# Layer 2 of a two-layer recurrent model: scaling of the gelu rows and their negative mean from VectorE to ScalarE, clipping later in VectorE's order

## The chip, the cores and the metric

The kernel runs on one core of a Trainium2 chip. The metric is the device time of one execution in microseconds, the median of several runs. TensorE multiplies matrices and transposes, VectorE, ScalarE and GpSimd work on rows, and SyncE's queue starts most transfers.

## What is computed

Two layers over 2048 tokens (2 x 1024) of width 256. Layer 1 is an attention with a mixture of 64 experts beside it. Layer 2 is a small attention whose output is gated by a feed-forward net with quantised activations. The part that matters here is that net:

```python
def absmax_quant(x):
    gamma = jnp.max(jnp.abs(x), axis=-1, keepdims=True)
    x_hat = jnp.clip(x * Q_B / gamma, -Q_B + EPS, Q_B - EPS)
    return x_hat * gamma / Q_B

def bitlinear(x, w):
    xn = layer_norm(x)
    x_hat = absmax_quant(xn)          # straight-through form left out
    w_hat = ternarize_weights(w)
    return jnp.einsum('bsd,od->bso', x_hat, w_hat)

h = bitlinear(x, w_fc)                # 256 -> 1024
h = jax.nn.gelu(h, approximate=False)
return bitlinear(h, w_proj)           # 1024 -> 256
```

Then `x = x + s * silu(ffn)`. The 1024-wide rows after gelu are normalised, scaled by 128 over their largest magnitude, clipped at 128 and multiplied with ternary weights.

## The kernel before

The program has one hand-written instruction list for each engine, and semaphores between them. There is no scheduler: the order is that of the code. Up to some 303 us of the profiled execution it works on layer 1; what follows is layer 2.

Layer 2 takes the 16 tiles of 128 tokens in pairs, p = 0 to 7 (`NP` = 8, `GT` = 2 tiles each). Every engine runs the loop `for p in range(NP + 2)` with several stages in flight. For one pair the stages are these, with the lines of the profile:

- GpSimd adds up the layer-1 result: `total` (line 467), `add_gated` (473, 474), signal `x1_ready`.
- VectorE normalises and quantises the 256-wide rows: `moments` (1115 to 1123), and `scales_and_rows`, which mixes Newton steps for reciprocal square roots (1094 to 1102) with the row steps `quantise` (1136 to 1147). Line 1147 is the last, with the signal `xq_ready`. It works two pairs ahead.
- TensorE transposes (`turn_q`, 1524), ScalarE copies the upper half to 16 bits (`high_q`, 713), VectorE takes the rest (`low_q`, 1174), and TensorE multiplies (`qkv`, 1538, `fc`, 1547).
- ScalarE computes gelu with a row sum (732) into `hid`. VectorE makes the negative mean (`means`, 1184), ScalarE squares the centred rows with a row sum (`square`, 738), VectorE takes their maximum (`spreads`, 1190, 1191) and, after the Newton steps, the scale and the bias (`hidden_scales`, 1194 to 1203).
- VectorE scales and shifts `hid` in place (`quantise_hidden`, 1211, two tiles) and clips it (1214, two tiles, signal `clip_ready`).
- ScalarE rounds to 16 bits (`high_hidden`, 753), GpSimd subtracts to get the rest (`low`, 502), TensorE transposes both (`turn_hidden`, 1576), ScalarE copies them out (`take_hT`, 745, 746), and TensorE multiplies (`down1`, 1587).
- ScalarE takes a tanh (`gate2`, 783), VectorE the product (`silu2`, 1221), GpSimd the last product and sum (`finish`, 510, 511), and SyncE stores.
- The small attention lies beside it: GpSimd `score_products` (483 to 489) and `attend` (496, 498), VectorE 1179, ScalarE 759, 763, 776, and TensorE `turn_att` (1558) and `project` (1566).

GpSimd's order in a round is: `total`, `attend`, `finish` twice, `add_gated`, `score_products`, `low` twice. ScalarE's ends with `take_hT`, two squares and two `high_hidden`. VectorE's is: line 1179, `spreads`, `moments`, `scales_and_rows`, `hidden_scales`, `silu` (1108), `means`, `quantise_hidden`, `product_scales`, `low_q`.

Of the kernel before, what the change touches and what calls it, by code (L numbers as in the profile page):

```python
# [54 lines left out]
GT = 2  # L55
# [18 lines left out]
def build(nc, q, Wk, bk, Wv, bv, Wo, bo, rw, eb, wg, wu, wd, sg, su, sd, wqkv, wpo, wfc, wpj, out):  # L74
# [9 lines left out]
    with ExitStack() as ctx:  # L84
# [107 lines left out]
        def l1(n):  # L192
# [88 lines left out]
                             "hi_ready", "lo_ready", "hT1_ps", "hT1_ready")]  # L281
        clip_ready = sem("clip_ready")
        z_ps, ztanh_ready, zu_ready, out_ready, out_stored = [sem(n) for n in (
# [254 lines left out]
        def _(sc):  # L538
# [187 lines left out]
            def gelu(n):  # L726
# [3 lines left out]
                if n >= 2 * GT:  # L730
                    sc.wait_ge(lo_ready, n - 2 * GT + 1)
                sc.activation(hid[n // GT % 2][:, q_, :], two[1][:, :], ACT.Gelu, scale=fcscale[n // GT % 2][:, q_:q_ + 1],  # L732
                              accum_out=hsum[:, q_:q_ + 1]).then_inc(gelu_ready, 1)

            def square(n):
                q_ = n % GT
                sc.wait_ge(nmean_ready, n // GT + 1)
                sc.activation(sq[q_], hid[n // GT % 2][:, q_, :], ACT.Square, bias=nmean[:, q_:q_ + 1], scale=1.0,
                              accum_out=ssq[:, q_:q_ + 1]).then_inc(sq_ready, 1)
# [57 lines left out]
            high_q(1)  # L797
            gelu(1)
            for q_ in range(GT):
                square(q_)  # L800
            for p in range(NP + 2):
# [23 lines left out]
                if p < NP:  # L825
                    for q_ in range(GT):
                        if p + 1 < NP:
                            square(GT * (p + 1) + q_)
                    for q_ in range(GT):
                        high_hidden(GT * p + q_)  # L830

        @block.vector
        def _(ve):
# [346 lines left out]

            def means(p):
                ve.wait_ge(gelu_ready, GT * p + GT)
                ve.wait_ge(dve, step[0])
                ve.tensor_scalar(nmean[:, :], hsum[:, :], -1.0 / FF1, None, ALU.mult).then_inc(nmean_ready, 1)

            def spreads(p):
# [6 lines left out]
            def hidden_scales(p):  # L1193
                mark(ve.tensor_scalar(hscale[:, :], ny[:, 3 * GT:], QB, None, ALU.mult))
                got = mark(ve.tensor_tensor(tmpc[:, :], nv[:, 3 * GT:], ny[:, 3 * GT:], ALU.mult))
                ve.wait_ge(dve, got - 1)
                mark(ve.tensor_tensor(hbias[:, :], hscale[:, :], nmean[:, :], ALU.mult))
                ve.wait_ge(dve, got)

                if p >= 2:  # L1200
                    ve.wait_ge(ztanh_ready, GT * (p - 1))
                    ve.wait_ge(s1_ready, p - 1)
                ve.scalar_tensor_tensor(out=zhalf[p % 2][:, :], in0=tmpc[:, :], scalar=gwc[:, 1:2], in1=ny[:, 2 * GT:3 * GT],
                                        op0=ALU.mult, op1=ALU.mult).then_inc(zhalf_ready, 1)

            def quantise_hidden(p):

                rows = [hid[p % 2][:, q_, :] for q_ in range(GT)]
                ve.wait_ge(dve, step[0])
                for q_, h in enumerate(rows):  # L1210
                    last = mark(ve.tensor_scalar(h, h, hscale[:, q_:q_ + 1], hbias[:, q_:q_ + 1], ALU.mult, ALU.add))  # L1211
                ve.wait_ge(dve, last)
                for h in rows:
                    ve.tensor_scalar(h, h, QB, -QB, ALU.min, ALU.max).then_inc(clip_ready, 1)
# [22 lines left out]
            low_q(1)  # L1237
            means(0)
            for p in range(NP + 2):
# [8 lines left out]
                if p + 3 < NP:  # L1248
                    silu(p + 3)
                if p + 1 < NP:  # L1250
                    means(p + 1)
                if p < NP:
                    quantise_hidden(p)
                if p + 2 < NP:
                    product_scales(p + 2)
                    low_q(p + 2)
                if p >= NP:
                    for q_ in range(GT):
# [382 lines left out]
```

## Time and profile before

| what | us |
|---|---|
| median of three runs | 491.08 |
| the three runs | 488.03, 491.08, 493.98 |
| span of the profiled execution, first to last instruction | 487.5 |
| VectorE busy in the span | 323.2 (66%) |
| GpSimd busy | 311.5 (64%) |
| ScalarE busy | 242.7 (50%) |
| TensorE busy | 374.0 (77%) |

The profiled execution's own device time is not given beside its span. The span is of one execution, the median of three others or the same. Busy time counts an instruction from its start to its end, whatever it does in between. A timeline row gives the start, the time taken, the engine, the line and what is written from what; an idle time and what ended it stand in brackets.

### The profile page before, as it was taken

Reading aid. Unit: us, or ns where it says so; the run is one execution under the profiler, and the core shown is the slowest. Engines: PE = TensorE matmul, PEld = TensorE weight load, DVE = VectorE, ACT = ScalarE, POOL = GpSimd, SP = SyncE. Lnnn points to the kernel's source line nnn. Section 1 sums busy time; section 2 is a strip of 40 time slices with the busy share of each in tenths; the row PEclk is TensorE's granted clock in tenths of the full one; section 3 lists DMA queues with packets and bytes.
Section 4 is the critical chain, followed back from the end, with each engine's and each line's share of the span. In section 5 each row is a group of like instructions: output and inputs, shape, how many; then the busy total and the mean of one; then the engine's idle time right before and its main releaser. Section 6 shows DMA issues by size and latency. Waiting matters only on the chain.

```text
span 487.5 us, 7393 instructions
## 1 busy us (share of the span) xinstructions
PE 374.0 (77%) x2246; PEld 282.0 (58%) x2246; DVE 323.2 (66%) x924; ACT 242.7 (50%) x542; POOL 311.5 (64%) x306
## 2 busy tenths in 40 slices
PE   0999969779998978978998973266676876779673
PEld 0974435566786756867786852133464663556562
DVE  6629892656555443556475631578999999999930
ACT  1344332624343436433344432327686967879661
POOL 6440005277877776788888874733957966968872
PEclk9999986899999999999899999678898989999797
DMA  7940055978889999778788556800000000000000
GB/s 250 339 136 0 1 150 185 274 178 182 211 178 209 244 226 217 144 167 181 159 202 179 94 68 109 281 0 0 2 0 11 13 24 1 23 22 12 13 32 32
DMA packets 58873, 57.90 MB, mean 119 GB/s; under 512 B 7099, under 2 KB 56531, under 8 KB 58835
## 3 DMA queue, kind: packets, MB, share of 16 engines
q1 hardware_dynamic: 46547, 38.55, 26.5%
q0 software_dynamic: 12288, 18.88, 21.1%
q8 instruction: 18, 0.29, 0.3%
q14 instruction: 20, 0.16, 0.1%
HBM read 39.69 MB, written 17.73 MB: 118 GB/s over the span
## 4 chain that ended last, share of the span: by engine, by line
DVE 33%; PE 30%; issue 12%; DMA 11%; POOL 8%; ACT 3%; SPq 1%; POOLq 0%; ACTq 0%; DVEq 0%
DMA acc_d<-W,idxE 7%; DVE W L1211 4%; DVE nv L1190 3%; PE two L1447 3%; POOL acc_d L459 3%; PE two L1307 3%; PE two L1363 3%; PE two L1273 3%; PE two L1459 2%; DMA W<-tok_d,idxE 2%; DVE nv L1191 2%; PE two L1399 2%; POOL W L439 2%; PE two L1321 2%; PE two L1436 2%
## 5 line engine op out<-in xcount | busy, mean ns | idle before, releaser
L459 POOL DMA_INDIRECT acc_d<-W,idxE x64 | 102.3, 1599 | 28.5 <-issue 14.8
L439 POOL DMA_INDIRECT W<-tok_d,idxE x56 | 56.6, 1010 | 61.4 <-DMA tok_d<-F 44.6
L1056 DVE SCALAR_TENSOR_TENSOR W<-W,two 128x88 f32<-128x88 f32 x64 | 15.6, 244 | 58.7 <-ACT W L679 35.4
L663 ACT ACTIVATE W<-two 128x256 f32<-128x256 f32 x64 | 24.4, 382 | 52.9 <-PE two L1436 50.8
L1547 PE MATMUL two<-wfcT,F 128*128 128x512 f16 x128 | 31.8, 393 | 6.3 <-ACT W L732 6.3
L502 POOL TENSOR_TENSOR F<-W,F 128x1024 f16<-128x1024 f32 x16 | 33.8, 2131 | 3.0 <-ACT F L753 2.4
L1033 DVE TENSOR_SCALAR W<-two,W 128x256 f32<-128x256 f32 x56 | 26.8, 479 | 12.6 <-DMA acc_d<-W,idxE 4.7
L1399 PE MATMUL two<-A,v 128*128 128x128 f32 x256 | 31.5, 276 | 4.4 <-issue 4.1
L1436 PE MATMUL two<-ident,W 128*128 128x128 f32 x112 | 24.0, 297 | 13.8 <-DMA W<-tok_d,idxE 11.1
L1399 PEld LDWEIGHTS two<-A,v 128*128 128x128 f32 x256 | 30.7, 192 | 6.3 <-issue 5.7
L1436 PEld LDWEIGHTS two<-ident,W 128*128 128x128 f32 x112 | 19.2, 201 | 25.7 <-DMA W<-tok_d,idxE 16.5
L1447 PE MATMUL two<-W 128*128 128x176 f32 x160 | 31.9, 324 | 0.2 <-ACT W L670 0.2
L1363 PE MATMUL two<-kT,vT 128*128 128x512 f32 x64 | 30.8, 604 | 0.0
L1587 PE MATMUL two<-wpjT,F 128*128 128x256 f16 x256 | 30.5, 280 | 0.0
L930 DVE TENSOR_REDUCE nmax<-two 128x1 f32<-128x1024 f32 x16 | 19.6, 1224 | 15.8 <-PE two L1363 13.8
L1587 PEld LDWEIGHTS two<-wpjT,F 128*128 128x128 f16 x256 | 25.7, 101 | 4.3
L510 POOL TENSOR_TENSOR F<-F 128x256 f32<-128x256 f32 x16 | 11.6, 727 | 22.8 <-DVE F L1221 22.8
L1459 PE MATMUL two<-W 88*128 88x256 f32 x80 | 25.1, 396 | 1.3 <-DVE W L1033 0.9
L1447 PEld LDWEIGHTS two<-W 128*128 128x128 f32 x160 | 25.4, 200 | 0.7 <-issue 0.7
L1576 PE MATMUL two<-ident,F 128*128 128x128 f16 x256 | 20.5, 244 | 5.8 <-POOL F L502 3.7
L1547 PEld LDWEIGHTS two<-wfcT,F 128*128 128x128 f16 x128 | 12.0, 101 | 20.1 <-ACT W L732 8.1
L1576 PEld LDWEIGHTS two<-ident,F 128*128 128x128 f16 x256 | 18.8, 111 | 8.2 <-POOL F L502 4.2
(230 smaller groups left out, 1035.3 us busy)
## 6 DMA issues: line engine op xcount, KB each, us to landing
acc_d<-xn SPq DMA_DIRECT2D x8, 512.0 KB
W<-in_L_ffn_w_gate SPq DMA_DIRECT2D x20, 176.0 KB
W<-in_L_ffn_w_up SPq DMA_DIRECT2D x20, 176.0 KB
W<-in_L_ffn_w_down SPq DMA_DIRECT2D x20, 176.0 KB
F<-in_L_ffn_w_gate SPq DMA_DIRECT2D x12, 176.0 KB
F<-in_L_ffn_w_up SPq DMA_DIRECT2D x12, 176.0 KB
F<-in_L_ffn_w_down SPq DMA_DIRECT2D x12, 176.0 KB
x<-in_L_attn_q SPq DMA_DIRECT2D x4, 512.0 KB, 5.6
```

The costliest lines, as they stand in the source:

```text
L439: pool.indirect_dma_start(out=xg[n % XR], out_offset=None, in_=tok_d[:, :], in_offset=bass.IndirectOffsetOnAxis(ap=idxE[:, n:n + 1], axis=0))\
L459: pool.indirect_dma_start(out=acc_d[n % 2][:, :], out_offset=bass.IndirectOffsetOnAxis(ap=idxE[:, n:n + 1], axis=0), in_=ysb[n % YS], in_o ...
L502: pool.tensor_tensor(lo16[n % GT], hid[n // GT % 2][:, n % GT, :], hi16[n % GT], ALU.subtract)\
L1033: ve.tensor_scalar(ysb[n % YS], bk_(3)[:, 0:D], xg[n % XR][:, D + n:D + n + 1], 0.5, ALU.mult, ALU.mult)\
L1363: ins = pe.matmul(two[2][:, 512 * h:512 * h + 512], vT[:, rows], kT[:, at:at + 512], start=True, stop=True)
L1399: ins = pe.matmul(bk_(1)[:, 0:P], v[:, (ORDER[t] // NP) * NP + i, :], probT[t % 2][:, i, :], start=(i == 0), stop=(i == 7))
L1436: ins = pe.transpose(bk_(2)[:, P * k:P * k + P], xg[n % XR][:, 0:D].rearrange("p (n k) -> p k n", k=KH)[:, k, :], ident[:, :])
L1447: ins = pe.matmul(gu[n % 2].rearrange("p (m f) -> p m f", m=2), xgT[n % 2][:, k, :], wgu[r][:, n % WG, :, k, :], start=(k == 0), stop=(k = ...
L1459: pe.matmul(bk_(3)[:, 0:D], hT[n % 2], wdn[(n // WG) % WR][:, n % WG, :], start=True, stop=True)\
L1547: ins = pe.matmul(bk_(2 + h), part[:, n % GT, k, :], wfcT[:, k, 512 * h:512 * h + 512], start=(i == 0), stop=(i == 3))
L1576: ins = pe.transpose(bk_(b).bitcast(F16)[:, P * k:P * k + P], part[n % GT][:, P * k:P * k + P], ident16[:, :])
L1587: ins = pe.matmul(bk_(7)[:, D * (n % GT):D * (n % GT) + D], part[n % 2][:, P * k:P * k + P], wpjT[:, k, :], start=(i == 0), stop=(i == 2 * ...
```

## The change

In layer 2, ScalarE gets two new steps. `scale_hidden` scales and shifts a tile of `hid` in place with one activation, once VectorE signals `hbias_ready`. `means` forms the negative mean there. VectorE's `quantise_hidden` only clips, each tile once `u_ready` says that it is scaled, and it stands after `product_scales` and `low_q` instead of before. The squares of the next pair follow ScalarE's new steps.

```diff
--- before.py
+++ after.py
@@ -279,7 +279,7 @@
         fc_ps, gelu_ready, nmean_ready, sq_ready, zhalf_ready, hi_ready, lo_ready, hT1_ps, hT1_ready = [
             sem(n) for n in ("fc_ps", "gelu_ready", "nmean_ready", "sq_ready", "zhalf_ready",
                              "hi_ready", "lo_ready", "hT1_ps", "hT1_ready")]
-        clip_ready = sem("clip_ready")
+        clip_ready, hbias_ready, u_ready = [sem(n) for n in ("clip_ready", "hbias_ready", "u_ready")]
         z_ps, ztanh_ready, zu_ready, out_ready, out_stored = [sem(n) for n in (
             "z_ps", "ztanh_ready", "zu_ready", "out_ready", "out_stored")]
 
@@ -732,9 +732,21 @@
                 sc.activation(hid[n // GT % 2][:, q_, :], two[1][:, :], ACT.Gelu, scale=fcscale[n // GT % 2][:, q_:q_ + 1],
                               accum_out=hsum[:, q_:q_ + 1]).then_inc(gelu_ready, 1)
 
+            def means(p):
+
+                sc.wait_ge(gelu_ready, GT * p + GT)
+                sc.activation(nmean[:, :], hsum[:, :], ACT.Copy, scale=-1.0 / FF1).then_inc(nmean_ready, 1)
+                sc.wait_ge(nmean_ready, p + 1)
+
+            def scale_hidden(n):
+
+                q_ = n % GT
+                sc.wait_ge(hbias_ready, n // GT + 1)
+                h = hid[n // GT % 2][:, q_, :]
+                sc.activation(h, h, ACT.Identity, bias=hbias[:, q_:q_ + 1], scale=hscale[:, q_:q_ + 1]).then_inc(u_ready, 1)
+
             def square(n):
                 q_ = n % GT
-                sc.wait_ge(nmean_ready, n // GT + 1)
                 sc.activation(sq[q_], hid[n // GT % 2][:, q_, :], ACT.Square, bias=nmean[:, q_:q_ + 1], scale=1.0,
                               accum_out=ssq[:, q_:q_ + 1]).then_inc(sq_ready, 1)
 
@@ -796,6 +808,7 @@
             gelu(0)
             high_q(1)
             gelu(1)
+            means(0)
             for q_ in range(GT):
                 square(q_)
             for p in range(NP + 2):
@@ -824,7 +837,10 @@
                     take_hT(GT * (p - 1) + 1)
                 if p < NP:
                     for q_ in range(GT):
-                        if p + 1 < NP:
+                        scale_hidden(GT * p + q_)
+                    if p + 1 < NP:
+                        means(p + 1)
+                        for q_ in range(GT):
                             square(GT * (p + 1) + q_)
                     for q_ in range(GT):
                         high_hidden(GT * p + q_)
@@ -1178,11 +1194,6 @@
                 ve.wait_ge(prod_ready, p + 1)
                 ve.tensor_reduce(dif[:, :].rearrange("p (g r) -> p g r", r=REP1), pr, AX.X, ALU.add).then_inc(dif_ready, 1)
 
-            def means(p):
-                ve.wait_ge(gelu_ready, GT * p + GT)
-                ve.wait_ge(dve, step[0])
-                ve.tensor_scalar(nmean[:, :], hsum[:, :], -1.0 / FF1, None, ALU.mult).then_inc(nmean_ready, 1)
-
             def spreads(p):
 
                 for q_ in range(GT):
@@ -1194,7 +1205,8 @@
                 mark(ve.tensor_scalar(hscale[:, :], ny[:, 3 * GT:], QB, None, ALU.mult))
                 got = mark(ve.tensor_tensor(tmpc[:, :], nv[:, 3 * GT:], ny[:, 3 * GT:], ALU.mult))
                 ve.wait_ge(dve, got - 1)
-                mark(ve.tensor_tensor(hbias[:, :], hscale[:, :], nmean[:, :], ALU.mult))
+                ve.wait_ge(nmean_ready, p + 1)
+                ve.tensor_tensor(hbias[:, :], hscale[:, :], nmean[:, :], ALU.mult).then_inc(hbias_ready, 1)
                 ve.wait_ge(dve, got)
 
                 if p >= 2:
@@ -1205,12 +1217,9 @@
 
             def quantise_hidden(p):
 
-                rows = [hid[p % 2][:, q_, :] for q_ in range(GT)]
-                ve.wait_ge(dve, step[0])
-                for q_, h in enumerate(rows):
-                    last = mark(ve.tensor_scalar(h, h, hscale[:, q_:q_ + 1], hbias[:, q_:q_ + 1], ALU.mult, ALU.add))
-                ve.wait_ge(dve, last)
-                for h in rows:
+                for q_ in range(GT):
+                    h = hid[p % 2][:, q_, :]
+                    ve.wait_ge(u_ready, GT * p + q_ + 1)
                     ve.tensor_scalar(h, h, QB, -QB, ALU.min, ALU.max).then_inc(clip_ready, 1)
 
             def silu2(n):
@@ -1235,7 +1244,6 @@
                     silu(2)
                     low_q(0)
             low_q(1)
-            means(0)
             for p in range(NP + 2):
                 if p < NP:
                     score_difference(p)
@@ -1247,13 +1255,11 @@
                     hidden_scales(p)
                 if p + 3 < NP:
                     silu(p + 3)
-                if p + 1 < NP:
-                    means(p + 1)
-                if p < NP:
-                    quantise_hidden(p)
                 if p + 2 < NP:
                     product_scales(p + 2)
                     low_q(p + 2)
+                if p < NP:
+                    quantise_hidden(p)
                 if p >= NP:
                     for q_ in range(GT):
                         silu2(GT * (p - 2) + q_)
```

VectorE's order around the clip, in one of the middle rounds, before. `W` holds the gelu rows, `F` the smaller tiles, `two` is PSUM:

```order
L1197 TENSOR_TENSOR hbias<-hscale,nmean 128x2 [waits dve_seq]
L1203 SCALAR_TENSOR_TENSOR zhalf<-tmpc,gwc,ny 128x2 [waits s1_ready,ztanh_ready,dve_seq]
L1108 SCALAR_TENSOR_TENSOR F<-F,xn 128x512 [waits gate_ready]
L1184 TENSOR_SCALAR nmean<-hsum 128x2 [waits dve_seq,gelu_ready]
L1211 TENSOR_SCALAR W<-W,hscale,hbias 128x1024 [waits dve_seq]
L1211 TENSOR_SCALAR W<-W,hscale,hbias 128x1024
L1214 TENSOR_SCALAR W<-W 128x1024 [waits dve_seq]
L1214 TENSOR_SCALAR W<-W 128x1024
L1167 SCALAR_TENSOR_TENSOR kvscale<-amax,ny 128x2 [waits gelu_ready,qkv_ready]
L1169 SCALAR_TENSOR_TENSOR fcscale<-amax,gwc,ny 128x2
L1174 TENSOR_TENSOR F<-two,F 128x512 [waits qT_hi_ready]
```

and after the change, at the same place (lines below 735 move down by 10 to 16, so 1124 is the old 1108 and 1223 the old 1214):

```order
L1209 TENSOR_TENSOR hbias<-hscale,nmean 128x2 [waits nmean_ready,dve_seq]
L1215 SCALAR_TENSOR_TENSOR zhalf<-tmpc,gwc,ny 128x2 [waits s1_ready,ztanh_ready,dve_seq]
L1124 SCALAR_TENSOR_TENSOR F<-F,xn 128x512 [waits gate_ready]
L1183 SCALAR_TENSOR_TENSOR kvscale<-amax,ny 128x2 [waits gelu_ready,qkv_ready]
L1185 SCALAR_TENSOR_TENSOR fcscale<-amax,gwc,ny 128x2
L1190 TENSOR_TENSOR F<-two,F 128x512 [waits qT_hi_ready]
L1223 TENSOR_SCALAR W<-W 128x1024 [waits u_ready] x2
L1195 TENSOR_REDUCE dif<-F 128x16 [waits prod_ready]
L1201 TENSOR_REDUCE nv<-W 128x1 [waits sq_ready] x2
```

The two scalings and the mean are gone; the product scales and low_q come first, and the clips wait for `u_ready` right ahead of the next round's first instruction.

ScalarE's order at the end of a round, before:

```order
L745 ACTIVATE F<-two 128x1024 [waits z_ps,hT1_ps]
L746 ACTIVATE F<-two 128x1024
L738 ACTIVATE W,ssq<-W,nmean 128x1024 [waits nmean_ready] x2
L753 ACTIVATE F<-W 128x1024 [waits hT1_ps,clip_ready] x2
L759 ACTIVATE F<-F 128x256 [waits attT_ps]
```

and after (738 and 746 are the new mean and scaling; 750, 757, 758 and 765 the old 738, 745, 746 and 753):

```order
L757 ACTIVATE F<-two 128x1024 [waits z_ps,hT1_ps]
L758 ACTIVATE F<-two 128x1024
L746 ACTIVATE W<-W,hbias,hscale 128x1024 [waits hbias_ready] x2
L738 ACTIVATE nmean<-hsum 128x2 [waits gelu_ready]
L750 ACTIVATE W,ssq<-W,nmean 128x1024 [waits nmean_ready]
L750 ACTIVATE W,ssq<-W,nmean 128x1024
L765 ACTIVATE F<-W 128x1024 [waits hT1_ps,clip_ready] x2
```

Two scalings and a mean stand between the copies of the transposed rows and the squares; the squares and the roundings to 16 bits come after them.

## Rows read from the trace of the kernel before

**Rows 1.** The page's slices: VectorE's busy tenths in 40 equal parts of the span.

```profile
DVE  6629892656555443556475631578999999999930
```

**Rows 2.** Busy time in one full round of the second layer.

```profile
core 0: us, PE busy (x) PEld busy (x) DVE busy (x) ACT busy (x) POOL busy (x), PEclk, DMA share, GB/s
384.70:404.70 20.00, 14.91 (x108) 11.22 (x108) 19.79 (x45) 14.85 (x26) 16.07 (x17) 0.91 0.05 15
```

**Rows 3.** VectorE in that round, in order of time: start us, us taken, then what.

```profile
387.17 1.94 DVE L1191 TENSOR_SCALAR nv<-ssq 128x2 f32<-128x2 f32 x1
...
391.03 0.82 DVE L1136 TENSOR_SCALAR F<-x,mv 128x256 f32<-128x256 f32 x1
...
394.08 0.43 DVE L1147 TENSOR_SCALAR F<-F 128x512 f32<-128x512 f32 x1
...
398.36 1.84 DVE L1211 TENSOR_SCALAR W<-W,hscale,hbias 128x1024 f32<-128x1024 f32 x1
```

**Rows 4.** Line 1191 in the round from 330 us.

```profile
L1191 DVE TENSOR_SCALAR nv<-ssq x1: 159/159/159, 334.0 to 334.0; 128x2 f32<-128x2 f32 x1
```

**Rows 5.** GpSimd from 384 us on, in order of time.

```profile
384.86 4.23 POOL L502 TENSOR_TENSOR F<-W,F 128x1024 f16<-128x1024 f32 x2
...
390.97 0.73 POOL L498 TENSOR_TENSOR F<-F 128x256 f32<-128x256 f32 x1
...
404.86 4.22 POOL L502 TENSOR_TENSOR F<-W,F 128x1024 f16<-128x1024 f32 x2
```

**Rows 6.** Line 1147 in three other rounds.

```profile
338.22 0.43 DVE L1147 TENSOR_SCALAR F<-F 128x512 f32<-128x512 f32 x1
...
356.15 0.43 DVE L1147 TENSOR_SCALAR F<-F 128x512 f32<-128x512 f32 x1
...
432.42 0.43 DVE L1147 TENSOR_SCALAR F<-F 128x512 f32<-128x512 f32 x1
```

**Rows 7.** Line 502 in four other rounds.

```profile
346.93 4.21 POOL L502 TENSOR_TENSOR F<-W,F 128x1024 f16<-128x1024 f32 x2
...
440.21 4.23 POOL L502 TENSOR_TENSOR F<-W,F 128x1024 f16<-128x1024 f32 x2
...
454.36 4.21 POOL L502 TENSOR_TENSOR F<-W,F 128x1024 f16<-128x1024 f32 x2
...
467.40 4.21 POOL L502 TENSOR_TENSOR F<-W,F 128x1024 f16<-128x1024 f32 x2 [2.45 <-ACT F L753]
```

**Rows 8.** ScalarE in order of time; in brackets its idle time before.

```profile
341.00 1.14 ACT L738 ACTIVATE W<-W,nmean 128x1024 f32<-128x1024 f32 x1
...
360.48 1.15 ACT L738 ACTIVATE W<-W,nmean 128x1024 f32<-128x1024 f32 x1
...
385.05 0.20 ACT L763 ACTIVATE td<-dif 128x16 f32<-128x16 f32 x1
...
399.97 1.15 ACT L738 ACTIVATE W<-W,nmean 128x1024 f32<-128x1024 f32 x1
...
436.75 1.15 ACT L738 ACTIVATE W<-W,nmean 128x1024 f32<-128x1024 f32 x1
...
439.01 2.00 ACT L753 ACTIVATE F<-W 128x1024 f16<-128x1024 f32 x2
...
452.96 2.00 ACT L753 ACTIVATE F<-W 128x1024 f16<-128x1024 f32 x2 [0.23 <-DVE W L1214]
...
463.81 1.02 ACT L746 ACTIVATE F<-two 128x1024 f16<-128x1024 f16 x1
466.26 2.00 ACT L753 ACTIVATE F<-W 128x1024 f16<-128x1024 f32 x2 [1.44 <-DVE W L1214]
```

**Rows 9.** TensorE's lines 1524 and 1576 after idle time, in order of time.

```profile
394.56 0.99 PE L1524 MATMUL two<-ident,F 128*128 128x128 f32 x4 [3.38 <-DVE F L1147]
...
432.90 0.65 PE L1524 MATMUL two<-ident,F 128*128 128x128 f32 x4 [2.54 <-DVE F L1147]
...
456.54 1.89 PE L1576 MATMUL two<-ident,F 128*128 128x128 f16 x16 [2.37 <-POOL F L502]
```

## The prediction

> **What bounds the kernel now.** I read the page's slices first: VectorE reads 9 in almost every slice from 330 to 466 us [rows 1]. That is the second layer, so an edit that takes work off VectorE looks right. The busy times of one round say more: in 20.00 us VectorE is busy 19.79, GpSimd 16.07, ScalarE 14.85 [rows 2]. Then I read VectorE in order of time, and its busy time turns out to hold waits. Line 1191 works on two numbers per partition; it takes 0.159 us in the first round [rows 4] and 1.94 us here [rows 3]. Here it ends at 389.11, and GpSimd's pair of line 502 ends at 389.09 [rows 5]. Line 1136, 0.82 us, ends at 391.85, GpSimd's line 498 at 391.70. So a VectorE instruction of this sort stands still until GpSimd's current instruction is over.
>
> The Trainium skill, SBUF — State Buffer, "Who interferes with whom", says that the two engines share a pair of ports as an exclusive lock, whoever starts first holding it for its whole instruction; the trace agrees (1.94 against 0.159 us). It names tensor_scalar and operations with two SBUF inputs as the VectorE side.
>
> This splits a round into two legs. Leg one runs from the first line 502 (the "low" subtraction, 384.86) to the end of line 1147 (394.51), which gives TensorE the next rows: 9.65 us, of the same length one round earlier (346.93 [rows 7] to 356.58 [rows 6]). It goes by GpSimd's string: two line 502, line 467, 496, 498; VectorE can do little until they are through. Taking work off VectorE leaves this leg as it is. Leg two runs from the end of line 1147 to the next line 502: 394.51 to 404.86 is 10.35 us. Line 502 needs ScalarE's line 753, and GpSimd must be through its own list.
>
> **The change, leg two by leg two.** S is the time from the end of line 1147 to ScalarE's first square (line 738); the two scalings go in there. Removed from VectorE per round: two line 1211 at 1.84 us or less (part of it waiting) and line 1184. Added to ScalarE ahead of the squares: two 1024-wide scalings and a two-element mean that the engine waits for itself. No row has a scaling with both scale and bias from memory. From below it is the plain line 753, two in 2.00 us, so 1.0 each. From above, and nearest in form, the squares: 436.75 to 439.01 is 2.26 for two [rows 8], 1.13 each. I take 1.13. The mean is like line 763, 0.20 us, plus about 0.1 (my estimate, half of that row) for the engine's wait on its own result: 0.3. Sum 2.56, lower end 2.2, upper end 2.9 (a tenth more for each scaling, twice the wait).
>
> The Trainium skill, ScalarE: Activation LUTs, "What ACT_TABLE_LOAD costs", gives 186 + 0.833 N ns, 93 more per pointer operand, 93 less back to back. With N = 1024 and two pointers that is an estimate of 1.13 us; with the plain copy's price the sum below would be some 2.5 us smaller.
>
> After S come 2.56 (new), 2.26 (squares) and then line 753 to line 502, which took 466.26 to 467.40 = 1.14. Line 502 is due at S + 5.96, by rows 8 and 7. The clip of line 1214, now after each scaling, waits beside the squares and hides there. The early product scales and low_q let TensorE start qkv and fc sooner; it waits for other things, so they cost nothing and bring ScalarE about 0.2 us once where its list is full. GpSimd's own list filled leg two to 10.35 us while it stood behind line 1211 and others. With one such wait (1.84 [rows 3]) gone it ends at 8.5, with none at 10.35. I take it to be under ScalarE's 9.9, since line 1211 came twice a round; at the upper end the three gains of 0.45 below are lost and the sum is 1.35 larger.
>
> - First leg two: S = 341.00 - 338.65 = 2.35 [rows 6, 8]; due at 8.31, was 8.28. Nothing.
> - Second: S = 360.48 - 356.58 = 3.90; due at 9.86, was 8.29: +1.6.
> - Third and fourth: was 10.35 each (the rows of the fourth stand for both). S was 399.97 - 394.51 = 5.46 with TensorE's line 1524 at 0.99 us after 3.38 idle, that is at 1.2 GHz; in the round of 432.90 it took 0.65 after 2.54 idle, at 2.4 GHz [rows 9], and S was 3.90. After the change I count some 2.6 us of idle ahead of it (fc now starts when gelu allows, and gelu moves with the squares). At 2.4 GHz: due at 9.9, -0.45 each. At 1.2 GHz: 11.4, +1.05 each.
> - Fifth: S as at 2.4 GHz: -0.45.
> - Sixth: end of line 1147 at 432.85; S = 436.75 - 432.85 = 3.90; due at 9.86. It was 440.21 - 432.85 = 7.36, because GpSimd has a short list: +2.5.
> - Seventh round (440.21 to 454.36): ScalarE had been busy from the line 753 at 439.01 to that at 452.96 but for little (0.23 before the latter). It gets 2.56 more, less that 0.23 and the 0.2 from above; line 502 then follows at once rather than behind GpSimd's list: +1.9 to 2.1.
> - Last round: line 746 ends at 464.83, line 753 started 466.26, 1.4 to 1.5 behind; now two scalings, 2.26: +0.7. Scaling and clipping overlap, but the first line 753 stands behind both scalings in ScalarE's order.
> - Before the first round, the first mean no longer crosses to VectorE and back: -0.2, an estimate from line 763's 0.20 us in rows 8.
>
> Sum at 2.4 GHz: 0 + 1.6 - 0.9 - 0.45 + 2.5 + 2.0 + 0.7 - 0.2 = +5.2. At 1.2 GHz in the third and fourth: +8.2. 2.6 us of idle lies close to the 2.54 that kept the clock, but line 1576 after 2.37 of idle ran its sixteen in 1.89 us, where the clock was low; I go a quarter of the way, +5.9. The span was 487.5 us; the profiled execution's own time isn't given apart, the lowest of the three runs is 488.03, the median 491.08. The addition lies wholly in the second layer, so I put it on the median: 497.0.
>
> **Rivals.** (a) Cheap scalings: 2.2 instead of 2.56, 0.36 less in the six leg twos that ScalarE ends and 0.26 in the last: +5.2 - 2.4 = +2.8, 493.9. For it: line 753. Against it: the squares have one operand from memory and take 0.13 more each.
> (b) Low clock in the third and fourth round: +8.2, 499.3. For it: 3.38 idle did it before, 2.37 may. Against it: gaps get shorter there.
> (c) VectorE sets the pace, and leg one shrinks. If its small instructions get through between GpSimd's, what leaves it is gained up to ScalarE's own pace: 14.85 + 2.56 = 17.4 a round. The five rounds from 346.93 to 440.21 took 93.3; five of 17.4 are 87.1: -6.2. The last two still give +2.0 + 0.7, the first -0.2: -3.7, 487.4, not slower and up to 1% faster. It decides from the point where VectorE reaches line 1136 before GpSimd's string starts. For it: 19.79 busy of 20.00. Against it: the pairs of equal ends in rows 3 and 5. The Trainium skill, Perfetto Trace Analysis, "Optimizing Scalar/DVE Operations", holds that moving work to ScalarE may pay if VectorE is saturated; that is this case, and whether VectorE is saturated or standing is what decides. Its ScalarE page, "Rules for kernel authors", says against the change that multiplies and adds belong on VectorE.
>
> **How the numbers follow.** The main case 0.42, own range 494.5 to 499; (a) 0.24; (b) 0.16; (c) 0.16; 0.02 for what I don't see. A measurement here tells about 1% from no change, 4.9 us. Slower by more: (b) and four fifths of the main case, 0.50. Faster by more: half of (c) and the rest, 0.10. The remainder 0.40 is within 1%. The range runs from (c) to just past (b): 488.5 to 500.
>
> **What would show it.** Right: line 1191 still ends with a line 502; leg one stays 9.65 us; the first line 502 starts about 9.9 us after line 1147 in every leg two from the second to the sixth; ScalarE's idle time after 440 us is gone; the scaling takes about 1.2 us from start to end. Wrong: leg one falls to 8 us or less (then (c)), or scalings near 1.05 us (then (a)), or line 1524 at 0.99 us (then (b)). The forecast fails as a whole if GpSimd's line 502 starts earlier in leg two than it did before in the sixth round.

## The result and the profile after

The changed kernel takes 496.24 us (median of four runs, 495.09 to 497.99) against 490.16 us for the kernel before, a ratio of 1.0113 with a 95% interval of 1.0079 to 1.0146. The forecast was 497.0, 5.9 us above the 491.08 known then. The change costs 5.5 us by the ratio and 6.1 by the two medians, just over 1%. The profiled execution took 495.68 us, its span 493.9. Ratios leave out single executions far slower than the others: among the twelve of the second measurement in experiment 1 one took 2008.79 us, which its median of 488.96 still counts (488.57 without it).

The page of the changed kernel, with the busy times and VectorE's slices:

```profile
PE 379.4 (77%) x2246; PEld 286.6 (58%) x2246; DVE 311.3 (63%) x900; ACT 260.2 (53%) x566; POOL 303.0 (61%) x306
...
DVE  6629991745554354656676540858969999986920
```

VectorE's busy time went from 323.2 to 311.3 us, ScalarE's rose from 242.7 to 260.2, and in VectorE's slices the unbroken row of nines [rows 1] now has eights and a six in it. VectorE got its relief and the kernel got slower.

The rounds, from GpSimd's first line 502 (the lower halves of the scaled rows) to the next. The timeline's columns are start, time taken, engine, line, output and input, and in brackets the idle time before and what ended it:

```profile
347.21 4.21 POOL L502 TENSOR_TENSOR F<-W,F 128x1024 f16<-128x1024 f32 x2 [0.18 <-ACT F L765]
...
367.72 4.21 POOL L502 TENSOR_TENSOR F<-W,F 128x1024 f16<-128x1024 f32 x2 [4.71 <-ACT F L765]
...
386.87 4.21 POOL L502 TENSOR_TENSOR F<-W,F 128x1024 f16<-128x1024 f32 x2 [0.37 <-ACT F L765]
...
407.01 4.21 POOL L502 TENSOR_TENSOR F<-W,F 128x1024 f16<-128x1024 f32 x2 [1.26 <-ACT F L765]
...
425.12 4.21 POOL L502 TENSOR_TENSOR F<-W,F 128x1024 f16<-128x1024 f32 x2 [0.37 <-ACT F L765]
...
443.23 4.21 POOL L502 TENSOR_TENSOR F<-W,F 128x1024 f16<-128x1024 f32 x2 [3.80 <-ACT F L765]
...
460.49 4.20 POOL L502 TENSOR_TENSOR F<-W,F 128x1024 f16<-128x1024 f32 x2 [4.97 <-ACT F L765]
...
474.23 4.21 POOL L502 TENSOR_TENSOR F<-W,F 128x1024 f16<-128x1024 f32 x2 [3.68 <-ACT F L765]
```

Where [rows 5] and [rows 7] had no wait ahead of line 502 but in the last round, now there is one in every round, and it is for ScalarE's line 765, the old 753. The other end of a leg is VectorE's line 1163, the old 1147, here in the timeline of the changed kernel, to be held against [rows 6] (those of 395.72 and 414.83 look the same):

```profile
339.11 0.43 DVE L1163 TENSOR_SCALAR F<-F 128x512 f32<-128x512 f32 x1
...
356.07 0.43 DVE L1163 TENSOR_SCALAR F<-F 128x512 f32<-128x512 f32 x1
...
376.58 0.43 DVE L1163 TENSOR_SCALAR F<-F 128x512 f32<-128x512 f32 x1
...
432.94 0.43 DVE L1163 TENSOR_SCALAR F<-F 128x512 f32<-128x512 f32 x1
```

Leg two runs from the end of such a row to the next line 502, leg one from there to the end of the next such row. With both sets of rows:

| | leg two before | after | my due time | leg one after it, before | after |
|---|---|---|---|---|---|
| first | 8.28 | 7.67 | 8.3 | 9.65 | 9.29 |
| second | 8.29 | 11.22 | 9.9 | 9.65 | 9.29 |
| third | 10.35 | 9.86 | 9.9 | 9.65 | 9.28 |
| fourth | 10.35 | 10.86 | 9.9 | 8.82 | 8.25 |
| fifth | 10.35 | 9.86 | 9.9 | 8.82 | 8.25 |
| sixth | 7.36 | 9.86 | 9.9 | | |

Round seven (443.23 to 460.49) takes 17.26 us, it was 14.15; the last (to 474.23) 13.74, it was 13.04. The legs two add 4.35 us, the legs one take away 2.23, the last two rounds add 3.81; the first line 1163 here ends 0.89 us later than the first line 1147 there, and what follows the last line 502 is 0.4 shorter. That makes the 6.4 us between the two spans. The 0.89 us lie ahead of the first added scaling (341.25), and such differences come without a cause in the code: in two profiles of one kernel (experiment 1) the first leg two starts at 338.75 and at 339.42, and its second and third line 1147 lie 15.09 and 13.90 us apart.

ScalarE's list in the sixth leg two of the changed kernel, and its wait in round seven:

```profile
437.27 2.37 ACT L746 ACTIVATE W<-W,hbias,hscale 128x1024 f32<-128x1024 f32 x2
439.54 0.20 ACT L738 ACTIVATE nmean<-hsum 128x2 f32<-128x2 f32 x1
439.76 1.15 ACT L750 ACTIVATE W<-W,nmean 128x1024 f32<-128x1024 f32 x1
...
442.05 1.99 ACT L765 ACTIVATE F<-W 128x1024 f16<-128x1024 f32 x2
...
451.08 1.11 ACT L732 ACTIVATE W<-two,fcscale 128x1024 f32<-128x1024 f32 x1 [1.54 <-issue]
```

The scalings start at 437.27, 3.90 us after line 1163 ended; that is S. Two scalings and the mean reach to the squares at 439.76, 2.49 (I had 2.56), the squares to 442.05, 2.29 (2.26), and line 502 follows at 443.23, 1.18 (1.14). Together 5.96, the number of the forecast. The rows of [rows 8] stood in the same order without the first two. The Trainium skill (ScalarE: Activation LUTs, "What ACT_TABLE_LOAD costs") has 186 + 0.833 N ns, 93 more for each pointer operand and 93 less back to back, from which 1.13 us for each scaling is an estimate. The trace agrees: from the first scaling to the mean's start it is 2.27 us for the two.

### The profile page after: what moved, and what is told of

Its sections match the earlier page's. It is cut to its first block and busy times, and to the rows that moved or that the text cites. A ratio compares the mean times of both kernels' runs of the same rounds, so it can differ in the third digit from the quotient of the medians.

```text
span 493.9 us, 7393 instructions
## 1 busy us (share of the span) xinstructions
PE 379.4 (77%) x2246; PEld 286.6 (58%) x2246; DVE 311.3 (63%) x900; ACT 260.2 (53%) x566; POOL 303.0 (61%) x306
## 5 line engine op out<-in xcount | busy, mean ns | idle before, releaser
L1553 PE MATMUL two<-wfcT,F 128*128 128x512 f16 x128 | 34.7, 420 | 11.7 <-ACT W L732 11.7
L1405 PE MATMUL two<-A,v 128*128 128x128 f32 x256 | 33.0, 284 | 6.4 <-issue 6.3
L1405 PEld LDWEIGHTS two<-A,v 128*128 128x128 f32 x256 | 32.0, 199 | 8.4 <-issue 7.8
L1582 PE MATMUL two<-ident,F 128*128 128x128 f16 x256 | 21.7, 252 | 17.6 <-POOL F L502 15.5
L1442 PEld LDWEIGHTS two<-ident,W 128*128 128x128 f32 x112 | 19.7, 201 | 21.7 <-DMA W<-tok_d,idxE 10.5
L946 DVE TENSOR_REDUCE nmax<-two 128x1 f32<-128x1024 f32 x16 | 19.6, 1223 | 16.3 <-PE two L1369 16.3
L510 POOL TENSOR_TENSOR F<-F 128x256 f32<-128x256 f32 x16 | 11.6, 724 | 20.4 <-DVE F L1230 20.4
```

Source lines behind the costliest of these rows:

```text
L1405: ins = pe.matmul(bk_(1)[:, 0:P], v[:, (ORDER[t] // NP) * NP + i, :], probT[t % 2][:, i, :], start=(i == 0), stop=(i == 7))
L1442: ins = pe.transpose(bk_(2)[:, P * k:P * k + P], xg[n % XR][:, 0:D].rearrange("p (n k) -> p k n", k=KH)[:, k, :], ident[:, :])
L1553: ins = pe.matmul(bk_(2 + h), part[:, n % GT, k, :], wfcT[:, k, 512 * h:512 * h + 512], start=(i == 0), stop=(i == 3))
L1582: ins = pe.transpose(bk_(b).bitcast(F16)[:, P * k:P * k + P], part[n % GT][:, P * k:P * k + P], ident16[:, :])
```

## The experiments

All ratios are to the kernel before, with runs of both on the same chip. The diffs are the parts that matter; new spare tiles and definitions are left out. A kernel goes by the number of its experiment. In the texts on record a kernel goes by its label, which stands in the heading of its experiment.

**1. The order alone (e1_order_only, and again e10_order_again).** This is the kernel before with another order. The scaling stays on VectorE; only the clip and the scaling move behind the product scales and low_q.

```diff
-                if p < NP:
-                    quantise_hidden(p)
                 if p + 2 < NP:
                     product_scales(p + 2)
                     low_q(p + 2)
+                if p < NP:
+                    quantise_hidden(p)
```

> The kernel before, with only VectorE's order changed: the scaling and the clip stay on VectorE but stand behind product_scales and low_q. Theory (ScalarE's list and TensorE's clock set the time from line 1147 to line 502): VectorE's clip ends about 1.3 us later, GpSimd's own list still fills 10.35 us in the third to fifth leg two, so those stay; the sixth goes from 7.4 to about 8.2 us. Total 0 to +2 us, ratio 1.000 to 1.004. Rival (VectorE's place in the chain is what counts, and the new order is what costs): most of the change's +6 us, ratio 1.008 or more.

Measured: 487.70 us, ratio 0.9947 (0.9897 to 0.9998). A second measurement beside another kernel:

> The kernel of e1_order_only once more, beside e9_hybrid_fill on the same chip, for the size of the order's gain. Theory: leg one 9.3 and 8.26 us, ratio to before 0.992 to 0.998. Rival: no gain, ratio 0.999 to 1.002, and the first measurement was chance.

Measured: 488.96 us, ratio 0.9943 (0.9906 to 0.998). So half of the change is a gain of half a per cent, which neither theory had. The legs two are nearly those of the kernel before (8.15, 8.16, three of 10.34, 7.88): the middle ones stay, as expected, and the sixth is 0.52 longer, where 0.8 was expected. The gain is in leg one: 9.30 and 8.26 instead of 9.65 and 8.82, as in the changed kernel. VectorE's timeline of this kernel in leg one:

```profile
385.81 0.36 DVE L1191 TENSOR_SCALAR nv<-ssq 128x2 f32<-128x2 f32 x1
...
390.18 0.82 DVE L1136 TENSOR_SCALAR F<-x,mv 128x256 f32<-128x256 f32 x1
...
392.88 0.43 DVE L1147 TENSOR_SCALAR F<-F 128x512 f32<-128x512 f32 x1
```

and GpSimd's:

```profile
384.01 4.22 POOL L502 TENSOR_TENSOR F<-W,F 128x1024 f16<-128x1024 f32 x2
...
390.11 0.73 POOL L498 TENSOR_TENSOR F<-F 128x256 f32<-128x256 f32 x1
```

Line 1191 takes 0.36 us here and ends as the first of the two line 502 is over (384.01 and 2.13 us later is 386.14, row end 386.17). Before, it started 2.31 us into the pair and stood until the second was over, 1.94 us [rows 3, 5]. The statistics of the next rows now lie beside the second line 502, and everything behind them comes earlier in VectorE's list. At the end of GpSimd's line 498 (390.84) it is the second of the two lines 1136 that comes free (ends 391.00), where before it was the first. The short one, 0.34 us, is done by then.

The changed kernel shows the same, VectorE first:

```profile
387.99 1.03 DVE L1202 TENSOR_SCALAR nv<-ssq 128x2 f32<-128x2 f32 x1
...
392.25 0.78 DVE L1152 TENSOR_SCALAR F<-x,mv 128x256 f32<-128x256 f32 x1
...
393.02 0.82 DVE L1152 TENSOR_SCALAR F<-x,mv 128x256 f32<-128x256 f32 x1
```

and the GpSimd row at which the last of them ends:

```profile
392.96 0.74 POOL L498 TENSOR_TENSOR F<-F 128x256 f32<-128x256 f32 x1
```

**2. Is it the lead that matters? (e8_late_reduce)** Kernel 1 with a maximum over 512 elements on VectorE ahead of line 1179, so that VectorE comes 0.6 us later.

```diff
                 if p < NP:
+                    ve.tensor_reduce(spare[:, p:p + 1], wpoT[:, :, :].rearrange("p k d -> p (k d)"), AX.X, ALU.max)
                     score_difference(p)
```

> The kernel of e1_order_only, with one more maximum over 512 elements (0.69 us) on VectorE ahead of line 1179 in each round. Theory (leg one is shorter in e1_order_only because VectorE reaches line 1191 before the first line 502 is over): that lead is lost, line 1191 stands until the second line 502 is over and leg one goes back to 9.65 and 8.82 us: +0.35 in the first four, +0.57 in the next, about 2 us over e1_order_only, ratio to before 0.997 to 1.001. Rival (leg one is VectorE's own work): +0.6 in every leg one, 3.5 us or more. Second rival (the lead doesn't matter): no change.

Measured: 491.78 us, ratio 1.0046 (1.0013 to 1.0078). Legs one are 9.63, 9.64, 9.64, 8.81 and 8.80. VectorE's timeline (its lines are one further down):

```profile
386.12 0.67 DVE L1242 TENSOR_REDUCE spare<-wpoT 128x1 f32<-128x512 f32 x1
...
389.30 1.86 DVE L1192 TENSOR_SCALAR nv<-ssq 128x2 f32<-128x2 f32 x1
...
393.07 0.82 DVE L1137 TENSOR_SCALAR F<-x,mv 128x256 f32<-128x256 f32 x1
...
396.12 0.43 DVE L1148 TENSOR_SCALAR F<-F 128x512 f32<-128x512 f32 x1
```

GpSimd's pair of line 502 in the same round:

```profile
386.91 4.22 POOL L503 TENSOR_TENSOR F<-W,F 128x1024 f16<-128x1024 f32 x2
```

The added instruction comes at 386.12, line 1191 (here 1192) starts 2.39 us into the pair and takes 1.86 again. 0.6 us of delay gave back 0.34 in the three longer legs and 0.55 in the two shorter ones. The rival had 0.6 in every leg; the shorter legs hardly tell the two apart, the longer ones do: there it is the place in GpSimd's string that counts. The total alone would have spoken for the rival: it is 4.1 us above the order alone by the medians and 4.9 by the ratios, where I expected 2. In the profiles the legs one add 2.1 us, and the sixth leg two another 0.97 (8.85 us, S at 5.40, TensorE at 1.2 GHz). Whether the delay had to do with that clock, and where the rest lies, stays open.

**3. The scalings left out (e2_no_scaling).** The changed kernel with one-element copies in place of ScalarE's two scalings, so the gelu rows aren't scaled.

```diff
-                sc.activation(h, h, ACT.Identity, bias=hbias[:, q_:q_ + 1], scale=hscale[:, q_:q_ + 1]).then_inc(u_ready, 1)
+                sc.activation(zlast[:, n:n + 1], hbias[:, q_:q_ + 1], ACT.Copy).then_inc(u_ready, 1)
```

> The kernel after, with ScalarE's two 1024-wide scalings replaced by one-element copies; the scaling of the gelu rows is left out. VectorE's and GpSimd's lists are those of the kernel after. Theory: 2.1 us less ahead of the squares in each round, so the sixth leg two falls from 9.9 to 7.8 us and round seven and the last fall by 2 each; the middle ones stop at GpSimd's list (8.5 to 9.5 us). Total 8 to 12 us below the kernel after, ratio to before 0.986 to 0.995. Rival (a) that the extra time of the change comes from VectorE's new waits and order: within 2 us of the kernel after, ratio 1.008 to 1.014.

Measured: 485.43 us, ratio 0.9876 (0.9828 to 0.9924), 10.8 us below the changed kernel by the medians and 11.6 by the ratios. ScalarE's list of the sixth leg two (its line 766 is the rounding):

```profile
433.50 0.30 ACT L747 ACTIVATE zlast<-hbias 128x1 f32<-128x1 f32 x2
...
433.92 1.15 ACT L751 ACTIVATE W<-W,nmean 128x1024 f32<-128x1024 f32 x1
...
436.20 1.99 ACT L766 ACTIVATE F<-W 128x1024 f16<-128x1024 f32 x2
```

GpSimd's line 502 after it:

```profile
437.39 4.22 POOL L503 TENSOR_TENSOR F<-W,F 128x1024 f16<-128x1024 f32 x2 [1.27 <-ACT F L766]
```

Line 1163 had ended at 429.60, so this leg two is 7.79 us, the expected 7.8. The third to fifth are 9.56 or 9.57 and no less, though ScalarE was ready: that is GpSimd's own list without the scalings on VectorE. The second is 9.15 with S at 5.26. Round seven falls by 3.4 us and the last by 1.3, where I expected 2 for each. VectorE's and GpSimd's lists are those of the changed kernel, so what the change costs is ScalarE's work.

**4. One scaling more (e3_third_scaling).** The changed kernel with a third scaling into a spare tile.

```diff
                         scale_hidden(GT * p + q_)
+                    sc.activation(spare[:, :], sq[1], ACT.Identity, bias=hbias[:, 1:2], scale=hscale[:, 1:2])
```

> The kernel after, with a third 1024-wide scaling into a spare tile on ScalarE in each round. Theory: +1.13 us in each leg two from the second to the sixth, in round seven and in the last, 0 to 1.1 in the first: +7 to +9 us over the kernel after, ratio to before 1.026 to 1.032. Rival (VectorE sets the pace, ScalarE has idle time in every round that takes it): 0 to +2 over the kernel after, ratio 1.011 to 1.016.

Measured: 507.27 us, ratio 1.0321 (1.0275 to 1.0367), 11.0 us above the changed kernel by the medians and 10.2 by the ratios. ScalarE's sixth leg two:

```profile
444.53 2.37 ACT L747 ACTIVATE W<-W,hbias,hscale 128x1024 f32<-128x1024 f32 x2
...
447.92 0.20 ACT L739 ACTIVATE nmean<-hsum 128x2 f32<-128x2 f32 x1
...
450.43 1.99 ACT L766 ACTIVATE F<-W 128x1024 f16<-128x1024 f32 x2
```

and GpSimd's line 502:

```profile
451.61 4.21 POOL L503 TENSOR_TENSOR F<-W,F 128x1024 f16<-128x1024 f32 x2 [5.72 <-ACT F L766]
```

From the first scaling to the mean is 3.39 us instead of 2.27, and from there to line 502 nothing changes (7.08 in all, 5.96 and 1.12). The first and the third leg two, with TensorE's clock as in the changed kernel, are 1.14 and 1.13 longer. The fifth and sixth are 1.6 longer: S is 4.35 and 4.40 there, behind a slow second fc (3.17 us for seven of its matmuls, 3.59 for eight). Round seven is 19.43 us, 2.2 longer. The total is 1 to 2 us over my 7 to 9. In the profiles the stretch from the first line 1163 to the last line 502 is 8.7 us longer, inside the forecast, and 3.0 us more lie ahead of it (342.51 against 339.54), before the first of the added scalings (346.49); what made those stays open. So ScalarE's time, which seemed free with 14.85 busy of 20 us [rows 2], is paid for at its full price.

**5. TensorE kept busy (e4_fill).** In the changed kernel, three places where TensorE stood idle read:

```profile
356.55 1.12 PE L1530 MATMUL two<-ident,F 128*128 128x128 f32 x4 [2.61 <-DVE F L1163]
...
396.21 0.66 PE L1530 MATMUL two<-ident,F 128*128 128x128 f32 x4 [2.39 <-DVE F L1163]
...
397.28 1.91 PE L1582 MATMUL two<-ident,F 128*128 128x128 f16 x16
...
447.76 3.23 PE L1553 MATMUL two<-wfcT,F 128*128 128x512 f16 x8 [1.29 <-ACT W L732]
```

Line 1530 (the old 1524) took 1.12 us in the second round. In the fourth it took 0.66, but the clock fell right behind it: it is 0.91 of the full one from 396.00 to 397.20 and 0.50 from 397.30 to 399.00, and line 1582 took 1.91 us for its sixteen, where the sixth leg two has 1.06. Line 1553 took 3.23 us for eight in round seven, where 1.89 is usual. The granted clock by round:

```profile
core 0: us, PE busy (x) PEld busy (x) DVE busy (x) ACT busy (x) POOL busy (x), PEclk, DMA share, GB/s
347.20:367.70 20.50, 15.45 (x107) 11.78 (x108) 15.44 (x41) 16.23 (x27) 11.25 (x12) 0.83 0.00 1
407.00:425.10 18.10, 13.91 (x113) 9.90 (x112) 17.31 (x41) 16.85 (x29) 14.10 (x15) 1.00 0.05 16
443.20:460.50 17.30, 12.05 (x87) 8.42 (x85) 12.88 (x24) 15.72 (x27) 10.38 (x14) 0.90 0.05 16
```

It is 0.83 of the full clock in the second round and 0.90 in round seven. The third and fourth rounds have 0.91 and 0.92, the fifth (shown) and the sixth 1.00. The experiment adds eight transposes of the identity at each of three places.

```diff
                 if 1 <= p <= NP:
+                    fill(8)
                     turn_hidden(GT * (p - 1))
                 if p + 1 < NP:
+                    fill(8)
                     fc(GT * (p + 1) + 1)
+                if p < NP:
+                    fill(8)
```

> The kernel after, with 8 transposes of the identity matrix on TensorE at each of three places where it stood idle (before turn_hidden, before the second fc, before turn_q). Theory: TensorE stays at 2.4 GHz, S in the second leg two falls from 5.3 to about 3.9 us, in the fourth from 4.9 to 3.9, and the second fc of round seven from 3.2 to 1.9 us: 3 to 4 us below the kernel after, less up to 1 us where a filler stands in the way, ratio to before 1.003 to 1.008. Rival (the lower clock is met by other slack): 0 to +2 us over the kernel after, ratio 1.011 to 1.016.

Measured: 493.58 us, ratio 1.0042 (1.001 to 1.0074), 3.5 us less than the changed kernel by the ratios. Two of its stretches, with the same columns:

```profile
349.10:368.30 19.20, 14.67 (x125) 11.38 (x124) 15.49 (x41) 16.17 (x27) 12.27 (x13) 1.00 0.01 1
443.10:459.50 16.40, 13.61 (x119) 11.16 (x117) 12.82 (x24) 15.80 (x27) 10.70 (x13) 1.00 0.05 17
```

The clock is full in the second to the seventh round, the second to sixth legs two are 9.85 or 9.86 all five, and round seven is 16.46. My main case had 16.1 for it and nothing but 9.9 for the legs: this is the kernel that I had computed. The two profiled executions alone don't show the gain: the spans are 494.1 and 493.9. From the first line 1163 to the last line 502 it is 3.25 us less, but the first line 1163 ends 1.9 us later and what follows the last line 502 is 1.6 us longer (21.2 against 19.7). That the fillers cost that 1.6 isn't shown; kernel 6, with the same fillers, has 20.1.

**6. Roundings first (e5_round_first_fill).** Kernel 5, with ScalarE's roundings ahead of the mean and the squares.

```diff
+                    for q_ in range(GT):
+                        high_hidden(GT * p + q_)
                     if p + 1 < NP:
                         means(p + 1)
                         for q_ in range(GT):
                             square(GT * (p + 1) + q_)
-                    for q_ in range(GT):
-                        high_hidden(GT * p + q_)
```

> The kernel of e4_fill (the change plus fillers on TensorE), with ScalarE's roundings (line 753 of before) ahead of the mean and the squares instead of behind them. Theory (line 502 starts a fixed stretch of ScalarE's list after S): the roundings start at S + 2.3, line 502 at S + 3.5 or at the end of GpSimd's own list: second leg two 9.9 to about 8, third to fifth 9.9 to 9.5, sixth 9.9 to 7.5 or 8; leg one back to 9.6 and 8.8, since the maxima come later. Together 3 to 4 us below e4_fill, ratio to before 0.995 to 0.999. Rival (what counts is ScalarE's total, wherever it stands): within 1 us of e4_fill, ratio 1.002 to 1.006.

Measured: 489.77 us, ratio 0.998 (0.9943 to 1.0018), 3 us below kernel 5 by the ratios. ScalarE's sixth leg two:

```profile
434.79 2.37 ACT L746 ACTIVATE W<-W,hbias,hscale 128x1024 f32<-128x1024 f32 x2
437.05 1.99 ACT L765 ACTIVATE F<-W 128x1024 f16<-128x1024 f32 x2
```

and GpSimd's line 502:

```profile
438.24 4.24 POOL L502 TENSOR_TENSOR F<-W,F 128x1024 f16<-128x1024 f32 x2 [1.30 <-ACT F L765]
```

The rounding starts at S + 2.26 and line 502 at S + 3.45; the leg is 7.36 us, as before the change. The second is 7.56, the third and fourth are 9.57 and 9.56. The fifth is 9.76 with S at 5.54, because a group of fillers stands ahead of line 1530 there. Leg one is 9.65, 10.05, 9.66, 8.82 and 8.82, since the maxima come late; my account has 9.65 for the second too. The same work costs nothing here, so its amount alone doesn't set the time in these rounds; what stands ahead of line 765 does. Round seven stays at 16.46: there it is the amount.

**7. Line 502 on half of the columns (e6_half_low).** Kernel 1, with the low parts of the other half left out.

```diff
-                pool.tensor_tensor(lo16[n % GT], hid[n // GT % 2][:, n % GT, :], hi16[n % GT], ALU.subtract)\
+                pool.tensor_tensor(lo16[n % GT][:, 0:512], hid[n // GT % 2][:, n % GT, 0:512], hi16[n % GT][:, 0:512], ALU.subtract)\
```

> The kernel of e1_order_only, with GpSimd's line 502 on half of the columns (the lower half of the low parts is computed, the rest left out). Theory (leg one goes by GpSimd's string): the pair of line 502 takes 2.1 us instead of 4.2, and leg one falls from 9.3 and 8.3 to about 7.2 and 6.4 us. Rival (leg one is VectorE's own work): leg one stays above 9.0 and 8.0 us.

Measured: 477.39 us, one run. GpSimd and VectorE in one leg one:

```profile
380.47 2.27 POOL L502 TENSOR_TENSOR F<-W,F 128x512 f16<-128x512 f32 x2
```

```profile
387.73 0.43 DVE L1147 TENSOR_SCALAR F<-F 128x512 f32<-128x512 f32 x1
```

The pair takes 2.27 instead of 4.22 us, and the leg (380.47 to 388.16) is 7.69 instead of 9.31; it followed by 1.6 of 1.95 us. Leg one goes by GpSimd's string for the most part, though less than I expected (7.2).

**8. The better half, and ScalarE where it is free (e7_hybrid, e9_hybrid_fill).** Kernel 1, with the two scalings on ScalarE for p = 2, 3 and 4 alone (`ON_ACT`). The diff leaves out VectorE's side, where these pairs are only clipped, once they are scaled; the mean stays on VectorE.

```diff
+                    if p in ON_ACT:
+                        scale_hidden(p)
                     for q_ in range(GT):
                         if p + 1 < NP:
                             square(GT * (p + 1) + q_)
```

> The kernel of e1_order_only (the clip late, the scaling on VectorE), with the two scalings on ScalarE in the pairs p = 2, 3, 4 alone, where GpSimd's own list was the later one; the mean stays on VectorE. Theory: third to fifth leg two from 10.34 to about 9.65 us (S + 5.7 or GpSimd's list at 9.5), all else as in e1_order_only: 2 us below it, ratio to before 0.988 to 0.993. Rival (ScalarE's scaling costs wherever it stands): 1 to 3 us above e1_order_only, ratio 0.997 to 1.002.

Measured: 486.63 us, ratio 0.9917 (0.9876 to 0.9958). GpSimd's line 502 of the third leg two, and TensorE's line 1524 (here 1543) at the start of the fourth:

```profile
384.31 4.22 POOL L502 TENSOR_TENSOR F<-W,F 128x1024 f16<-128x1024 f32 x2
```

```profile
393.66 1.12 PE L1543 MATMUL two<-ident,F 128*128 128x128 f32 x4 [2.38 <-DVE F L1157]
```

Line 1147 had ended at 374.69, so the third leg two is 9.62, with the fifth at 9.63, and 10.34 in kernel 1. The fourth is 11.25: there TensorE ran at 1.2 GHz after 2.38 us of idle. The second is 8.71 with S at 5.26, 8.16 in kernel 1. So I put the fillers in, up to the sixth round:

> The kernel of e7_hybrid with the fillers of e4_fill on TensorE in the rounds p = 0 to 5. Theory: TensorE at 2.4 GHz in all of them, S 3.9 in each, so the second leg two falls to GpSimd's 8.15 and the fourth from 11.25 to 9.65 us: 1.5 to 2.5 us below e7_hybrid, ratio to before 0.985 to 0.989. Rival (the fillers cost what they bring): ratio 0.990 to 0.995.

Measured: 486.98 us, ratio 0.9913 (0.9881 to 0.9946). Its third, fourth and fifth legs two are 9.62, 9.61 and 9.62. The second is 8.39, not 8.15: S is 4.93, so the fillers didn't keep the clock there. From the first line 1147 to the last line 502 the profile is 1.9 us shorter than that without fillers, but the median isn't less. That is the rival's side: the profiled execution without fillers had slow rounds that its other runs may not have had, or the fillers cost elsewhere; the runs don't tell. Kernels 8 with and without fillers are the fastest full versions here, 0.8 to 0.9% below the kernel before; that they beat the order alone (0.9943 to 0.9947) is within the intervals.

## Why the prediction was right

- **ScalarE's list ends leg two.** Right, and shown from both sides: less work 10.8 us faster (3), more work 11.0 slower (4), both by the medians, and the same work behind the rounding instead of ahead of it brings the sixth leg back to its 7.36 us (6).
- **The price of the added work, 2.56 us.** Measured 2.49. Rival (a), cheap scalings, falls.
- **S + 5.96.** Measured 5.96 in the sixth leg two, and all six legs two of the changed kernel are within 0.01 us of that once S is known (1.71, 5.27, 3.90, 4.90, 3.91, 3.90).
- **GpSimd's own list.** I put it under 9.9 us, between 8.5 and 10.35. Kernel 3 shows 9.56.
- **TensorE's clock.** The term was mis-sized. I took a quarter of two low rounds, 0.7 us, and put them at the third and fourth. They came at the second (S 5.27 instead of 3.90), the fourth (4.90) and as a slow fc in round seven (3.23 instead of 1.89). Against kernel 5 that is 1.4 + 1.0 + 0.8 = 3.2 us: of the 1.3 us in the fc, round seven lost only 0.8 (17.26 against 16.46). Kernel 5 is 3.5 us faster by the ratios. Round seven, forecast at +2.0, is +3.1: 0.8 is the clock, and the last 0.3 stand in kernel 5 too (+2.3).
- **"Taking work off VectorE leaves this leg as it is."** This step failed. Leg one fell by 0.36 us in three rounds and 0.57 in two, 2.2 in all. It goes by GpSimd's string, as kernel 7 shows, but where VectorE stands in its own list when the string begins decides how many of its instructions lie beside it. Kernel 2 takes the gain away with 0.6 us. It is rival (c) at a small scale, and it comes from the new order, not from the work taken off: kernel 1 has all of it.
- **The first leg two** was 0.6 us shorter, where I had nothing. S fell from 2.35 to 1.71 us, and that is TensorE's clock too. The kernel before shows, in its first leg two:

```profile
338.70 1.11 PE L1524 MATMUL two<-ident,F 128*128 128x128 f32 x4 [0.45 <-DVE F L1147]
```

The clock is 0.50 there; the changed kernel has 0.65 us for the same four. Kernel 1 has 0.66 and S at 1.72, kernel 2, with the same order, 1.12 and 2.40. So the early low_q isn't enough for it, and what decides the clock there stays open.

- **Last round, +0.7.** Measured +0.70.
- **The signs.** Line 1191 (now 1202) still ends with a line 502: 389.02, and the first line 502 of that round at 389.00. Three of the five legs two were 9.86, the other two longer by their S. Leg one didn't stay at 9.65. ScalarE's idle time after 440 us wasn't gone: 1.54 us stand ahead of 451.08, behind the slow fc; in kernel 5 it is 0.22. The range was said to start at (c), whose own sum is 487.4, but was put at 488.5.

The misses nearly cancel: -2.2 in the legs one and -0.6 in the first leg two against +2.5 for the clock and +0.3 in round seven. So it is luck that the total of 497.0 is so close to 496.24; its parts were further off. (In the profiles the start adds 1.1 us more than forecast and the end takes 0.4 away.)

The change is two edits with opposite signs. The order is worth -0.5% (1), and with ScalarE's work on top of it the whole is +1.1%, so that work costs about 1.7%, some 8 us.

## What to carry to other kernels

Busy time doesn't tell an engine that works from one that stands at a port: look at how long a two-element instruction takes (0.159 and 1.94 us here). An engine with a quarter of its time free can still be the one that everything waits for, if what is added stands ahead of the one result that another engine needs; look at the place first, then at the load. And split a change that both moves and reorders: here one half was a gain that the other half hid.

## What the runs showed of the hardware that I had not expected

A VectorE instruction that stands at the shared port gets in between two GpSimd instructions that follow each other without a pause: line 1191 in kernel 1 started inside the first line 502 and was over in 0.36 us as that ended, while the second went on after it. The Trainium skill (SBUF — State Buffer, "Who interferes with whom") has the lock for the length of an instruction, and the runs agree; that the waiting engine comes next, they add.

The granted clock didn't follow the length of the idle time just before. Line 1524 or its successor ran at 1.2 GHz after 2.61 us of idle (changed kernel, second round), after 2.38 (kernel 8) and after only 0.45 (the kernel before, 338.70). It ran at 2.4 GHz after 2.54 [rows 9], and in kernel 3 after 2.90:

```profile
429.65 0.66 PE L1531 MATMUL two<-ident,F 128*128 128x128 f32 x4 [2.90 <-DVE F L1164]
```

After 2.39 us (changed kernel, 396.21) line 1530 still ran at 2.4 GHz and the clock fell behind it. With the gaps filled the clock was full from the second to the seventh round of kernel 5, and 0.75 in its last; in kernel 8 the fillers left the second leg two with S at 4.93.
